# Four attention-like blocks on one core: early attentions tiled by queries, and some row maxima taken from key differences

## What is computed

```
L0: x1 = wp @ attention(q, k, v of groupnorm(x)) + bp + x         one head of width 128, softmax over 256 keys
L1: pam = gamma_pam * attention(q, k of width 16, v of 128)(x1) + x1
    cen = pam @ pam^T (channels by channels); att = softmax(max(cen) - cen); x2 = gamma_cam * (att @ pam) + pam
L2: q, k = (x2 joined with a fixed embedding) @ Wq, Wk; 8 heads of width 16, softmax over 256 keys; x3 = o @ Wout + bout + x2
L3: f = channel norm(x3); q, k, v = 3x3 depthwise conv(1x1 conv(f)); q = softmax over each head's width / 4,
    k = softmax over tokens; ctx = k^T v per head; out = channel norm(out_w @ silu(q ctx)) + x3;
    y = ff_w2 @ channel norm(gelu(ff_w1 @ channel norm(out))) + out
```

## Time and profile before

| | us |
|---|---|
| runs of the kernel before | 89.85, 88.72, 89.69 (median 89.69) |
| the profiled execution | 88.5 |
| its span, first to last instruction | 86.7 |
| PE busy | 73.4 (85%) |
| DVE busy | 59.5 (69%) |
| ACT busy | 46.0 (53%) |
| POOL busy | 30.0 (35%) |

### The profile page before, as it was taken

How to read it: one execution, slowest core, us unless ns; L and a number is a source line. 1 busy time by engine, 2 the same in 40 slices (tenths; PEclk the granted TensorE clock), 3 DMA queues, 4 the chain that set the end, 5 groups by cost and what they waited for, 6 DMA issues and landing times.

```text
span 86.7 us, 1617 instructions
## 1 busy us (share of the span) xinstructions
PE 73.4 (85%) x547; PEld 53.1 (61%) x547; DVE 59.5 (69%) x188; ACT 46.0 (53%) x123; POOL 30.0 (35%) x61
## 2 busy tenths in 40 slices
PE   4985999999999999738799899999999559677970
PEld 2244887586868767617373564599999338545740
DVE  1438678779486739794949732499999946797650
ACT  4100488439713244363737388798988633717630
POOL 7950250003970550000000003068888830363600
PEclk9999999999999999999999999999999999999997
DMA  2889700000000000000000000000000000000003
GB/s 19 237 261 358 293 6 0 0 0 8 0 4 0 0 0 0 4 0 8 0 0 0 0 8 0 0 0 0 0 0 11 0 0 0 4 0 0 0 0 121
DMA packets 1304, 2.91 MB, mean 34 GB/s; under 512 B 144, under 2 KB 784, under 8 KB 1296
## 3 DMA queue, kind: packets, MB, share of 16 engines
q1 hardware_dynamic: 1152, 2.68, 9.8%
q10 hardware_dynamic: 144, 0.13, 0.4%
HBM read 2.55 MB, written 0.26 MB: 32 GB/s over the span
## 4 chain that ended last, share of the span: by engine, by line
PE 49%; DVE 27%; ACT 8%; POOL 5%; issue 4%; DMA 3%; POOLq 0%; ACTq 0%
DVE nmx L683 11%; PE bank L1036 5%; POOL vacc L251 5%; DVE kacc L726 4%; DMA x<-in_x 3%; PE bank L849 3%; PE bank L1199 3%; PE bank L1209 2%; PE bank L939 2%; PE bank L960 2%; PE bank L890 2%; ACT pT L344 2%; PE bank L1179 2%; PE bank L967 1%; PE bank L1048 1%
## 5 line engine op out<-in xcount | busy, mean ns | idle before, releaser
L213 POOL TENSOR_TENSOR rs<-ve,mhalf 128x2 f32<-128x2 f32 x8 | 5.6, 698 | 28.0 <-DVE ve L490 27.8
L251 POOL TENSOR_TENSOR vacc<-vacc,vprod 128x240 f32<-128x240 f32 (+1 forms) x16 | 10.8, 676 | 5.6 <-ACT vprod L380 3.7
L344 ACT ACTIVATE pT<-bank 128x512 f32<-128x512 f32 x16 | 8.5, 601 | 7.8 <-PE bank L1063 7.8
L683 DVE TENSOR_REDUCE nmx<-bank 128x2 f32<-128x512 f32 x16 | 9.9, 686 | 3.6 <-PE bank L1036 3.6
L1130 PE MATMUL bank<-convw,fsh 128*128 128x128 f32 x72 | 9.0, 275 | 0.0
L1130 PEld LDWEIGHTS bank<-convw,fsh 128*128 128x128 f32 x72 | 8.6, 192 | 0.1
L229 POOL TENSOR_TENSOR convw<-wgc,tapw 128x128 f32<-128x128 f32 x9 | 4.1, 485 | 8.8 <-DVE wgc L639 8.8
L380 ACT ACTIVATE vprod<-bank,wc 128x256 f32<-128x256 f32 x16 | 6.5, 493 | 0.0
L726 DVE SCALAR_TENSOR_TENSOR kacc<-bank,wc,kacc 128x240 f32<-128x240 f32 (+1 forms) x16 | 6.3, 447 | 0.0
L857 PE MATMUL bank<-warm 128*128 128x512 bf16 x13 | 4.6, 501 | 1.2 <-DVE warm L496 1.2
L267 ACT ACTIVATE p<-bank,nmax 128x256 f32<-128x256 f32 x8 | 3.7, 473 | 2.4 <-DVE nmax L494 2.4
(11 more groups left out here) (207 smaller groups left out, 179.2 us busy)
## 6 DMA issues: line engine op xcount, KB each, us to landing
wc<-in_pack_c SPq DMA_DIRECT2D x1, 649.0 KB, 7.6
wb<-in_pack_b SPq DMA_DIRECT2D x1, 612.0 KB, 6.5
tapw<-in_taps SPq DMA_DIRECT2D x1, 576.0 KB, 8.5
wa<-in_pack_a SPq DMA_DIRECT2D x1, 320.0 KB, 4.0
out<-y SPq DMA_DIRECT2D x2, 128.0 KB, 1.7
x<-in_x ACTq DMA_DIRECT2D x1, 128.0 KB, 2.8
x<-in_x SPq DMA_DIRECT2D x1, 128.0 KB, 2.6
wa<-in_pack_a SPq DMA_DIRECT2D x1, 72.5 KB, 2.6
```

What stands on the lines that cost most here:

```text
L213: nc.gpsimd.tensor_tensor(dst, src, mhalf[:, 0:width], ALU.pow).then_inc(done, 1)
L251: nc.gpsimd.tensor_add(vacc[b][:, oy, ox], vacc[b][:, oy, ox], vprod[n - 1][b][:, iy, ix]).then_inc(s["vsum_d"], 1)
L344: nc.scalar.activation(pT2[u % PT2_RING][:, :, :], tiles(bank[SCORE_T_BANKS[u % HG]]), ACT.Exp).then_inc(s["e2_d"], 1)
L683: nc.vector.tensor_reduce(nmx2[g][:, :, col:col + 1], tiles(bank[SCORE_BANKS[i]]), AX.X, ALU.max, negate=True).then_inc(s["max2_d"], 1)
```

## The change

The line numbers change; those of the kernel before are used here and in the prediction, save in the rows of the order after.

1. **First attention by tiles.** Scores, maximum, exponential, transposes, copy and mix are separate stages per tile of 128 queries, in banks of their own, and stand interleaved in the lists.
2. **Second attention by tiles, in token rows.** q and k are made twice, in two row quadrants (`wqk`, made by POOL), so the two score products use different rows of the array. `mix1` gives tokens in rows, so 1/sum is a value per row: one instruction per tile (`pam_sum`) multiplies, adds the transposed residual (`xb1_transposes`, `xb1T_evac`) and writes pamT. `scale1`, `rb1_evac` and the two-step sum are gone; `pam_transposes` now turn pamT back into pam, behind `energy`.
3. **Maxima from differences.** POOL writes key differences k[128+j] - k[j] behind the keys (`key_steps`). In groups 1 to 3, heads 2 and 3 multiply the queries with the first 128 keys and the 128 differences. As max(a, b) = a + max(b - a, 0), ACT takes the positive part (`head_excess`, 128 x 256 per head), and DVE adds it to the first half and takes the extreme, with `tensor_tensor_reduce` of 128 x 128, two per head. Heads 0 and 1, and group 0, keep the 128 x 512 reduction. `k_max` becomes one such instruction of 128 x 256.
4. **Moves.** `ff_mean_1`, `ff_mean_2` and the DVE stages behind them stand near the end; the identity product of `x3_tokens` is a stage `x3_ident` ahead of it; the lists are reordered, among them three of batch 0's `v_sums` before batch 1's inverse root instead of two; D ** -0.5 is put into a mask by POOL.
5. Semaphores are merged or split; `q1` and `k1` are no longer cleared.

```diff
-        qm2, km2, qa2 = per_batch("qm2", [128, NG, N]), per_batch("km2", [128, NG, N]), per_batch("qa2", [128, NG, N])
+        qm2, km2, qa2 = per_batch("qm2", [128, NG, N]), per_batch("km2", [128, NG, N + 128]), per_batch("qa2", [128, NG, N])
+        PAIRED = {grp: (HG - 2, HG - 1) for grp in range(1, NB * NG)}
+        excess2, pairmax2 = ([sb(f"{n}_{i}", [128, NT, 128]) for i in range(2)] for n in ("excess2", "pairmax2"))
...
+        SCORE0, PROB_T0 = (3, 1), (0, 3)
+        SCORE1, PROB_T1, PAM = (2, 1), (0, 2), (3, 1)
...
+            nc.gpsimd.tensor_copy(wqk[:, :, :, :], B("wqkT1").rearrange("p (n r) -> p n r", n=2).unsqueeze(2).broadcast_to([128, 2, NT, QUAD])).then_inc(s["prep_w"], 1)
...
+            def key_steps(b):
+                for g in range(NG):
+                    if NG * b + g not in PAIRED:
+                        continue
+                    pool.wait_ge(s["k2_d"], NG * b + g + 1)
+                    nc.gpsimd.tensor_tensor(km2[b][:, g, N:N + 128], km2[b][:, g, 128:N], km2[b][:, g, 0:128], ALU.subtract).then_inc(s["kd2_d"], 1)
+
...
+            for stage, b in ((xb2_sum, 0), (key_steps, 0), (xb2_sum, 1), (key_steps, 1), (root3, 0), (v_sums(1, 4), 0), (root3, 1),
+                             (v_sums(4, TAPS), 0), (v_sums(1, TAPS), 1), (root4, 0), (root4, 1), (root5, 0), (root5, 1), (root6, 0),
+                             (root6, 1)):
...
+            def exp0(t):
+
+                def stage(b):
+                    act.wait_ge(s[f"max0_d{t}"], b + 1)
+                    nc.scalar.activation(p0[b][:, t, :], bank[4 * b + SCORE0[t]][:, 0:N], ACT.Exp, bias=nmax[b][:, t:t + 1],
+                                         accum_out=psums[b][:, t:t + 1]).then_inc(s[f"e0_d{t}"], 1)
+                return stage
+
...
-            def rb1_evac(b):
-                act.wait_ge(s["rb1_p"], b + 1)
-                nc.scalar.activation(rb1[b][:, :], bank[4 * b + 1][:, 0:N], ACT.Copy).then_inc(s["rb1_d"], 1)
...
+            def head_excess(g, i):
+
+                def stage(b):
+                    grp = NG * b + g
+                    act.wait_ge(s["s2_p"], grp * HG + i + 1)
+                    act.wait_ge(s["max2_d"], HG * grp)
+                    nc.scalar.activation(excess2[i - HG + 2][:, :, :], tiles(bank[SCORE_BANKS[i]])[:, :, 128:N], ACT.Relu).then_inc(s["ex2_d"], 1)
+                return stage
...
+            def max0(t):
+
+                def stage(b):
+                    dve.wait_ge(s[f"s0_p{t}"], b + 1)
+                    nc.vector.tensor_reduce(nmax[b][:, t:t + 1], bank[4 * b + SCORE0[t]][:, 0:N], AX.X, ALU.max,
+                                            negate=True).then_inc(s[f"max0_d{t}"], 1)
+                return stage
...
-            def pam_sum(b):
-                dve.wait_ge(s["pv1_p"], b + 1)
-                dve.wait_ge(s["rb1_d"], b + 1)
-                nc.vector.tensor_mul(t1[b][:, :], bank[4 * b + 3][:, 0:N], rb1[b][:, :]).then_inc(s["vec"], 1)
-                vec_done("n1")
-                dve.wait_ge(s["vec"], vec_at("n1", b + 1))
-                dve.wait_ge(s["vec"], vec_at("xb1", b + 1))
-                nc.vector.tensor_add(pam[b][:, :], t1[b][:, :], xb1[b][:, :]).then_inc(s["pam_d"], 1)
-
...
+            def pam_sum(t):
+
+                def stage(b):
+                    dve.wait_ge(s[f"pv1_p{t}"], b + 1)
+                    dve.wait_ge(s["rs1_d"], b + 1)
+                    dve.wait_ge(s["xb1T_d"], b + 1)
+                    nc.vector.scalar_tensor_tensor(pamT[b][:, t, :], bank[4 * b + PAM[t]][:, 0:C], rsum1[b][:, t:t + 1], xb1T[b][:, t, :],
+                                                   ALU.mult, ALU.add).then_inc(s[f"pamT_d{t}"], 1)
+                return stage
...
+                        if i in PAIRED.get(grp, ()):
+                            dve.wait_ge(s["ex2_d"], 2 * (grp - 1) + i - HG + 3)
+                            for t in range(NT):
+                                pair = nc.vector.tensor_tensor_reduce(pairmax2[i - HG + 2][:, t, :], tiles(bank[SCORE_BANKS[i]])[:, t, 0:128],
+                                                                      excess2[i - HG + 2][:, t, :], -1.0, 3.0e38, ALU.add, ALU.min,
+                                                                      nmx2[g][:, t, col:col + 1])
+                            pair.then_inc(s["max2_d"], 1)
+                        else:
+                            nc.vector.tensor_reduce(nmx2[g][:, :, col:col + 1], tiles(bank[SCORE_BANKS[i]]), AX.X, ALU.max,
+                                                    negate=True).then_inc(s["max2_d"], 1)
+                return stage
...
-                dve.wait_ge(s["vec"], vec_at("ktap", TAPS * (b + 1)))
-                nc.vector.tensor_add(kc[b][:, :], kacc[b][:, 0, :, :].rearrange("p h w -> p (h w)"),
-                                     kacc[b][:, 1, :, :].rearrange("p h w -> p (h w)")).then_inc(s["vec"], 1)
-                vec_done("kc")
-                dve.wait_ge(s["vec"], vec_at("kc", b + 1))
-                nc.vector.tensor_reduce(nmk[b][:, :], kc[b][:, :], AX.X, ALU.max, negate=True).then_inc(s["k3m_d"], 1)
...
+                for n in (TAPS - 1, TAPS):
+                    dve.wait_ge(s["vec"], vec_at(f"ktap{b}", n))
+                nc.vector.tensor_tensor_reduce(kc[b][:, :], kacc[b][:, 0, :, :].rearrange("p h w -> p (h w)"),
+                                               kacc[b][:, 1, :, :].rearrange("p h w -> p (h w)"), -1.0, 3.0e38,
+                                               ALU.add, ALU.min, nmk[b][:, :]).then_inc(s["k3m_d"], 1)
...
+                    rows = slice(QUAD * t, QUAD * (t + 1))
+                    nc.tensor.matmul(bank[4 * b + SCORE1[t]][:, 0:N], q1[b][rows, t * 128:(t + 1) * 128], k1[b][rows, :],
+                                     start=True, stop=True, tile_position=(QUAD * t, 0)).then_inc(s["s1_p"], 1)
...
+                if grp in PAIRED:
+                    pe.wait_ge(s["kd2_d"], grp)
...
+                            keys = km2[b][rows, g, :].rearrange("p (s k) -> p s k", s=3)[:, 0:3:2, :]
...
+            def x3_ident(b):
+
+                pe.wait_ge(s["xb2_d"], b + 1)
+                pe.wait_ge(s["oe2_d"], NG)
+                if b:
+                    pe.wait_ge(s["e2_d"], 3 * HG + 2)
+                for t in range(NT):
+                    nc.tensor.matmul(LA[b][:, t * C:(t + 1) * C], xb2[b][:, t * 128:(t + 1) * 128], ident, start=(t == 0), stop=False,
+                                     skip_group_check=True)
...
```

More of the change, by code:

```diff
@@ L111, in build @@
         p1, pT1 = p0, pT0
[L112 removed]
+        pam = per_batch("pam", [128, N])
         pamT = per_batch("pamT", [128, NT, C])
@@ L925, in row_scale, with p0_transposes, stage @@
+            def p0_transposes(t):
+                def stage(b):
+                    for i in range(t + 1):
+                        pe.wait_ge(s[f"e0_d{i}"], b + 1)
+                    prob_transposes(bank[4 * b + PROB_T0[t]], p0[b], t, s[f"t0_p{t}"])
+                return stage
             def row_scale(b, rs, rb_p):
@@ L964, in embedding, with xb1_transposes @@
+            def xb1_transposes(b):
+                pe.wait_ge(s["q1_d"], b + 1)
+                pe.wait_ge(s["k1_d"], b + 1)
+                pe.wait_ge(s["xb1_d"], b + 1)
+                for t in range(NT):
+                    last = nc.tensor.transpose(bank[4 * b][:, t * C:(t + 1) * C], xb1[b][:, t * 128:(t + 1) * 128], ident)
+                last.then_inc(s["xb1T_p"], 1)
             def embedding(n):
                 def stage(b):
+                    pe.wait_ge((s["pam_d"], s["ce_d"])[n], b + 1)
@@ new lines, in mix1, with stage @@
+            def mix1(t):
+                def stage(b):
+                    pe.wait_ge(s["v1_d"], b + 1)
+                    pe.wait_ge(s[f"pT1_d{t}"], b + 1)
+                    for i in range(NT):
+                        last = nc.tensor.matmul(bank[4 * b + PAM[t]][:, 0:C], pT1[b][:, i, t * 128:(t + 1) * 128], v1[b][:, i, :],
+                                                start=(i == 0), stop=(i == NT - 1))
+                    last.then_inc(s[f"pv1_p{t}"], 1)
+                return stage
@@ L984, in pam_transposes @@
             def pam_transposes(b):
[L985 removed]
                 for t in range(NT):
[L987 to L988 removed]
+                    pe.wait_ge(s[f"pamT_d{t}"], b + 1)
+                    last = nc.tensor.transpose(bank[4 * b][:, t * 128:(t + 1) * 128], pamT[b][:, t, :], ident)
+                last.then_inc(s["pam_p"], 1)
@@ L990, in energy @@
             def energy(b):
-                pe.wait_ge(s["pamT_d"], b + 1)
+                for t in range(NT):
+                    pe.wait_ge(s[f"pamT_d{t}"], b + 1)
                 for t in range(NT):
```

498 lines of the change are left out of this document (265 added, 233 removed).

## The result

The changed kernel takes 84.77 us, the median of four runs (84.54 to 85.11), beside 89.2 for the kernel before in the same session; the ratio is 0.951, 95% interval 0.941 to 0.960. That is 4.4 us less. Run again later it took 84.73, ratio 0.958 (0.956 to 0.961). The profiled execution took 85.11 us with a span of 83.0 (before 88.5 and 86.7). Executions of the kernel before at a granted clock of 0.98 or 0.96 take 89.6 us and more, those at 0.99 to 1.0 take 88.3 to 88.7, so two of the first session's four, 89.69 and 89.85, look like slow ones, and at like clock the gain is 88.50 - 84.73, about 3.8 us.

A forecast was written before the change was run, and what follows sets the result against it. Bounds: PE in front, a VectorE-PE cycle in grouped attention, POOL's additions in the third block, then a tail. 0.56 + 2.6 + 0.0 + 1.0 = 4.2 off 89.69 gives 85.5 us; own range 84.8 to 86.4, whole 83.8 to 87.6.

The forecast's parts named there:

- First attention, 0.56: First attention: with the new order the mix ends at 14.13 and the sum starts about 14.17, not 14.73; 0.56 us off.
- From x1 to the grouped scores, 2.6: Front, x1 to group scores: less PE work and two hidden waits take 2.6 us off, between 1.72 and 3.47.
- I take the middle of floor and ceiling: Front: gain set at 2.6 us, between 1.72 with waits unchanged and 3.47 with both waits hidden and nothing new.
- The two plain waits: Front: PE's waits for VectorE's two-step sum (1.15 us) and for x2 (some 0.6 us) would be covered by other work.
- PE idle for more than 2 us: Sign of a wrong prediction: PE idle for over 2 us between x1 and the grouped scores.
- Grouped attention, 0.0: Grouped attention: four instruction pairs (1.24 us) replace two reductions (1.25) per group in three groups; no change.
- a pair as 0.31: Grouped attention: main instruction plus partly overlapped read-out costs 0.31 us, within bounds of 0.21 to 0.44.
- rival (e): Grouped attention: changed maxima don't shorten the cycle because scores and transposes close it anyway; 0.0, no separate chance given.
- Third block, 0.7: Third block: earlier f of batch 0 and three additions before batch 1's root move POOL's last addition 0.7 us earlier.
- one addition of 0.79 leaves the run of fourteen: Third block: a third POOL addition fits the 0.77 us wait before batch 1's root, shortening the later run.
- Tail, 0.4 - 0.1 = 0.3: After POOL's last addition: batch 0's statistics follow 0.4 us sooner, while centred weights delay batch 1 by 0.1 uncovered.
- Rival (c): Front comes near its ceiling, 3.4 us, or a pair costs 0.25; 84.7 us, chance 0.09.

The follow-up runs named there:

- the pairs alone: Kernel before plus only the maxima from differences for two heads of groups 1 to 3; 88.16 us beside 88.50 for the kernel before.

## Why the prediction was right, point by point

85.5 us was forecast and 84.77 measured: faster by more than 2% as expected, within the whole range of 83.8 to 87.6, but 0.03 below the 84.8 at which the likeliest case's own range begins. The sum of 4.2 stands beside 3.90 of the body and 3.8 of the times at like clock, so it was a little too high. That the forecast time is nevertheless 0.7 above the measured one comes from its base, 89.69, which is 1.2 above the 88.5 of the profiled execution that the sum was read from; 88.5 - 4.2 = 84.3 would have been 0.4 too low. The two errors point in opposite ways and partly cancel, and so do errors among the terms: that is luck.

**First attention, 0.56: measured 0.38.** The count of PE's work was right: 2.82 forecast from the end of the scores to the end of the mix, 2.94 measured (11.57 to 14.51). The rest is a semaphore's time ahead of the sum. What the step did not see is how much the release by tiles carries: without it the changed order is 1.43 slower, in this stretch a whole microsecond slower than the kernel before.

**From x1 to the grouped scores, 2.6: measured 2.1.** The floor of 1.72 for work left out held. That the work left out gives it is counted from the rows of both kernels (the row scale and the weight means are gone from the stretch, and two score products have one row of 0.63); no run puts that work back. The step that was too high is "I take the middle of floor and ceiling". From 15.63 to 29.25 are 13.62 us with 11.45 of work, so 2.17 of waiting instead of 2.55. The two plain waits did go, but the shorter stages lose time at eleven places for 0.1 to 0.25 each: in the chain's rows 0.24 at each product of q and k, 0.20 and 0.15 at scores and residual transposes of each batch, 0.25 and 0.10 at each energy product, 0.21 at the first mix, 2.1 in sum. Whether late data or the wait itself costs this, no run here tells apart. The check marks were late accordingly: the minimum at 23.27 for "near 22", x2 at 25.85 for 25, the group scores at 29.25 for 28.3. The sign "PE idle for more than 2 us" of a wrong prediction isn't there by the profile's count, which has 0.20 of idle time, but the 2.17 beyond the work is just what it was meant to catch.

**Grouped attention, 0.0: measured 0.7.** The mis-sized term is "a pair as 0.31". It is 0.21, the lower bound of my own range; a group gains 0.37, and a cycle is 3.81 where I had said 4.1 to 4.3. I had reasoned from ScalarE's read-out and so counted a part of the read-out. What argued for the upper bound, the rule to keep the number of instructions small in the Trainium skill, VectorE: DVE Perf Modes, Rules for kernel authors, is not borne out here: eight instructions take 0.88 (2.13 less 1.25 for the two reductions left) where two took 1.25. Three times 0.37 is 1.1, of which 0.7 is on the chain, by the run without pairs, since after group 2 PE's list closes the cycle. Of these 0.7, 0.48 is left at the end of the body. That part of rival (e) is true of the third group. ScalarE and POOL hid their share as I had said; the pairs never waited long.

**Third block, 0.7: more at its entry, less at its end.** Of the 1.46 between group scores and first addition the pairs are 0.7. The other 0.76 is left for the residual product and the mixed transposes that moved; I tested no one of them alone. The step that failed is "one addition of 0.79 leaves the run of fourteen", which took the 0.77 us for time "in which POOL now waits". In the kernel before POOL is at work there, on the root itself:

```profile
58.43 0.70 POOL L213 TENSOR_TENSOR rs<-ve,mhalf 128x2 f32<-128x2 f32 x1
```

Between its first and last addition it is idle only for the 0.14 or so between two instructions, so an addition that changes its place shortens nothing there. In the changed order the third addition fills a hole of 0.56 ahead of the root, but it holds up VectorE's small addition by 0.4 and so the root behind it, and is worth 0.22 by the run with two. Then POOL pauses for 0.46, of which 0.2 is on the path. And its ninth addition, the first of batch 1, starts at 60.15, 0.08 behind ScalarE's copy (60.07), and 0.14 after the eighth; in the kernel before it starts 0.04 ahead of the eighth's end, so 0.19 more is lost to late copies. "Merging the maximum saves about 0.3, off the path" was wrong in place: it is on the path and saves 0.47, since ScalarE's copies for POOL, the one for the ninth addition first, are behind the exponential that waits for it. That figure is from one run.

**Tail, 0.4 - 0.1 = 0.3: measured 0.28.** The statistics of batch 0 start 2.29 behind the last addition (66.87 to 69.16) instead of 2.65, 0.36 of the 0.4. The weights' 0.1 is 0.0: they put 0.4 on the chain, and the product of batch 1 would hold GELU as long. I had named "GELU waits for POOL's root" as a sign of a wrong prediction; it is there, and the run with the weights later shows it costs nothing.

So first attention, front and third block fell short by 0.18, 0.5 and 0.28 (0.76 - 0.34 is 0.42, for 0.7), and the pairs brought 0.7 instead of nothing: 3.9 instead of 4.2. The medians of the first session fell by 0.5 more than the body; at like clock the difference is 3.8, and nothing is left over. **Rival (c)** named a pair of 0.25 or a front near its ceiling and 84.7 us; the cheap pair came, the front did not. Its 84.7 is nearest to the measured time, but it is added up from the front at 3.4 and from the same base of 89.7, so that is luck, too.

## What to carry to other kernels

Splitting a stage into tiles pays by its earlier release, and in this kernel a small stage behind a wait cost PE 0.1 to 0.25 us again: count the places where the new list waits, not only the work it leaves out. A saving on a cycle counts only in the turns where that engine closes it; here two of three. An engine named as the cause of a wait can be innocent: give the data earlier, and see whether the wait stays.

## What the runs showed of the hardware

- **VectorE and POOL hold each other up.** A VectorE addition of two columns takes 0.17 us, and 0.29 or 0.56 when POOL's addition is under way, ending as that one ends. The maximum of k's taps, with two inputs in SBUF, takes 0.43 or 0.89, a plain addition in its place 0.42 or 0.93, and qn 0.42, 0.65 or 0.69. POOL is held, too: its additions, mostly 0.60 to 0.71, take 0.82 (kernel before, from 60.69) and 0.79 (kernel after, from 64.49) where VectorE's instruction at the maximum of k's taps began 0.1 to 0.15 ahead. In the Trainium skill, SBUF — State Buffer, Who interferes with whom, the two engines share a port pair that one of them holds for a whole instruction; a VectorE instruction with two inputs in SBUF contends for it with a POOL instruction that reads SBUF, and so does one in a 2-port mode, which reads one tensor through both ports. The traces agree that the second to come waits, in both directions; they don't show the mode of the small addition, which has one input. The multiply-adds of k's taps, with one input in PSUM, take 0.43 to 0.46 beside POOL's additions. The pairs are no test, as POOL stands idle while they run.
- **POOL pauses for 0.46 to 0.49 us at one place of its list**, where 0.14 is usual. It stays behind the tenth addition when the data come earlier or an addition moves past the root, sits after the ninth in the kernel before with three more instructions, and is gone from the changed kernel without its three key differences or with 24 clears more. A fixed number of instructions ahead does not explain it alone: with three fewer it should come three additions later, and the gap there is 0.14. The profiles have a few transfers of instructions, but none from 60 to 62.6 us in the run with two additions, whose pause is 61.77 to 62.25, and none from 55 to 65 in the pairs alone, whose pause is 64.01 to 64.48. So the cause stays open.
- **An accumulating VectorE pair of 128 x 128 costs 0.21 us** in a row of such pairs. A main instruction lasts 0.286 and its read-out 0.084, but the next main instruction starts 0.21 after the last one, at the same time as the read-out.
